# Order of weight loads and gate stores on the loading queue of an eight-expert feed-forward stage

## The reference

```python
xn = _layernorm(x, axis=-1)
s  = _L1_attn_ref(xn, wq, bq, wk, bk_, wv, bv, wo, bo)
gate = einsum('becd,edf->becf', xn, w1)      # 8 experts, d = 256, f = 704
up   = einsum('becd,edf->becf', xn, w3)
out  = einsum('becf,efd->becd', silu(gate) * up, w2)
x = x + s * silu(out)
```

## Time and profile before

| | us |
|---|---|
| median of 3 runs | 2246.42 |
| the 3 runs | 2246.42, 2250.37, 2243.02 |
| span of the profiled execution, first to last instruction | 2244.4 |
| TensorE matmul busy | 1996.7 (89%) |
| VectorE, ScalarE, GpSimd busy | 1538.4, 1396.0, 685.8 |

### The profile page before, as it was taken

How to read it: one execution, slowest core, us unless ns; L and a number is a source line. 1 busy time by engine, 2 the same in 40 slices (tenths; PEclk the granted TensorE clock), 3 DMA queues, 4 the chain that set the end, 5 groups by cost and what they waited for, 6 DMA issues and landing times. The chain is left out here.

```text
span 2244.4 us, 41413 instructions
## 1 busy us (share of the span) xinstructions
PE 1996.7 (89%) x12160; PEld 1485.8 (66%) x12160; DVE 1538.4 (69%) x3292; ACT 1396.0 (62%) x3261; POOL 685.8 (31%) x1032
## 2 busy tenths in 40 slices
PE   2999999999999999999999777787499999999997
PEld 1777768767777687687777566676355566656653
DVE  5886885877858858858778543232477777777773
ACT  3675675675756756757667544333267877777784
POOL 0343443433433434434434213233200210111012
PEclk9999999999999999999999888899699999999999
DMA  6000000000000000000000271211200110110001
GB/s 216 1 0 19 0 0 19 0 0 19 0 10 10 0 19 0 0 19 0 0 10 0 85 273 50 96 53 55 92 19 1 48 42 5 47 47 15 32 28 38
DMA packets 52360, 76.87 MB, mean 34 GB/s; under 512 B 1856, under 2 KB 42688, under 8 KB 51776
## 3 DMA queue, kind: packets, MB, share of 16 engines
q1 hardware_dynamic: 51744, 75.05, 9.7%
q10 hardware_dynamic: 544, 1.05, 0.2%
HBM read 55.12 MB, written 20.97 MB: 34 GB/s over the span
## 5 line engine op out<-in xcount | busy, mean ns | idle before, releaser
L1539 DVE TENSOR_REDUCE nm<-ps 128x1 f32<-128x512 f32 x512 | 336.9, 687 | 114.1 <-PE ps L1398 110.2
L826 POOL TENSOR_SCALAR pr<-pr,rinv 128x128 f32<-128x128 f32 (+3 forms) x512 | 262.8, 532 | 409.4 <-DVE rinv L700 409.4
L1650 ACT ACTIVATE pt<-pst 128x512 f32<-128x512 f32 x512 | 296.1, 602 | 142.0 <-PE pst L1406 140.9
L557 ACT ACTIVATE pr<-sc,nmax 128x128 f32<-128x128 f32 (+3 forms) x512 | 263.7, 530 | 88.0 <-DVE nmax L689 88.0
L832 POOL TENSOR_TENSOR qk<-ra,rb 128x256 f32<-128x256 f32 x256 | 195.3, 774 | 275.2 <-DVE rb L713 236.3
L1398 PE MATMUL ps<-kb,qb 96*128 96x512 f32 x512 | 238.0, 467 | 12.5 <-DVE nm L1539 10.0
L404 PE MATMUL w<-ident,pr 128*128 128x128 f32 x1280 | 194.3, 286 | 41.2 <-DVE qs L720 25.6
L689 DVE TENSOR_REDUCE nmax<-sc 128x1 f32<-128x128 f32 (+3 forms) x512 | 216.4, 482 | 19.9 <-PE sc L392 19.7
L390 PE MATMUL sc<-k,qs 128*128 128x256 f32 (+2 forms) x512 | 212.3, 416 | 12.4 <-DVE k L727 11.2
L1406 PE MATMUL pst<-qb,kb 128*128 128x512 f32 x512 | 208.0, 408 | 6.7 <-ACT pt L1650 3.6
L404 PEld LDWEIGHTS w<-ident,pr 128*128 128x128 f32 x1280 | 139.7, 144 | 81.7 <-DVE qs L720 43.4
(11 more groups left out here) (207 smaller groups left out, 5079.3 us busy)
## 6 DMA issues: line engine op xcount, KB each, us to landing
raw<-in_w SPq DMA_DIRECT2D x16, 704.0 KB, 8.0
raw<-in_w SPq DMA_DIRECT2D x8, 640.0 KB, 6.5
xa<-in_x SPq DMA_DIRECT2D x2, 2048.0 KB, 13.7
x<-in_x SPq DMA_DIRECT2D x8, 512.0 KB, 3.5
x_scratch<-x SPq DMA_DIRECT2D x8, 512.0 KB, 3.6
xt_hi_scratch<-xt_hi SPq DMA_DIRECT2D x1, 4096.0 KB, 14.7
xt_lo_scratch<-xt_lo SPq DMA_DIRECT2D x1, 4096.0 KB, 23.5
gate_scratch<-go SPq DMA_DIRECT2D x32, 128.0 KB
```

The lines of the kernel that those rows point to most:

```text
L557: act.activation(pr[:, h, SOFF[i]:SOFF[i] + (i + 1) * P], sc[:, bank, at:at + (i + 1) * P], ACT.Exp, bias=nmax[:, h, i:i + 1], accum_out=r ...
L826: pool.tensor_scalar(p, p, rinv[:, h, i:i + 1], 1.0, ALU.mult, ALU.mult).then_inc(scaled, 1)
L1539: dve.tensor_reduce(nm[:, g % 2, i, h:h + 1], ps[:, i % 2, :], AXX, ALU.max, negate=True).then_inc(max_done, 1)
L1650: act.activation(pt[:, g % 2, h, i, :], pst[:, i % 2, :], ACT.Exp).then_inc(exp_done, 1)
```

## The change

In the loop of the loading queue the two calls change places. For each e from 0 to 5 SyncE now issues the weights of expert e+2 first (with the four waits of `load13` and `load2` ahead of them) and the four stores of expert e second. The loads and stores, their waits, their sizes and all other engines' programs stay as they are.

```diff
                 sp.dma_start(io.xt1_lo, c.xt1_lo[:].bitcast(F32)).then_inc(xt_stored, 16)
                 with sp.Fori(0, E1 - 2) as e:
+                    load(e + 2)
                     store(e)
-                    load(e + 2)
                 store(E1 - 2)
                 store(E1 - 1)
                 sp.wait_ge(g_stored, 16 * NT * E1)
```

## The result

The changed kernel takes 2187.89 us (median of 4 runs, 2186.28 to 2188.42), the kernel before 2244.72 us beside it (2240.6 to 2250.37): a ratio of 0.974, with a 95% interval of 0.973 to 0.976. The forecast was 2185.4 us, with a range of 2180 to 2193.

The account below looks back on a forecast made before the run. The prediction took TensorE in experts 1 to 6 to be held by w1's load queued behind four stores; removing that gains 61.0 us, other terms cost 0: 2246.4 - 61.0 = 2185.4 us, range 2180 to 2193.

Parts of the forecast that it names:

- What bounds the kernel: Experts 1 to 6: ScalarE's first w1 cast (L1006) waits for a load behind four stores, stopping TensorE 47.6 us.
- When the load leaves: L944 of load(e+2) issues when w3 of expert e+1 is split, at 1322.8 instead of 1336.96.
- When it lands: Raw w1 tile for experts 1 to 6: between 3.9 and 11.31 us after issue, upper end taken, so 1334.1.
- e = 0, behind the stores of xt1: First load(e+2), while xt1 is still being stored: lands between 1333.0 and 1340.4; cost 0, at most about 0.2 us.
- The HBM figure of 358 GB/s: Objection for e = 0: 2.66 + 1.44 MB would take 11.5 us and land at 1334.2, the sum unchanged.
- The 3.64 us that TensorE bears: A cast starting by 1340.27, against ScalarE ready at 1336.63, does not stop TensorE in block 4.
- The stores behind the loads: The 24 loop stores (L965) finish by 1346, ScalarE needs them (L1026) at 1355.4: cover 9 us.
- slower rival: Stores behind 2.1 MB of loads hold ScalarE at L1026; one period late costs 94 us less 61: 2279; chance 0.02.
- The number of engines: Gate stores use 2 DMA engines, their slowest dimension, agreeing with DMA share 0.13, 2.1 of 16 engines.
- The sum: Expert 0's go to expert 6's go: 210.93 less six periods of 24.98 us gives 61.05 us gained.
- The second count: Cross-check over six experts: TensorE's idle 47.6 us plus 15 us of block 4 at lower clock makes 63.
- The median: Whole kernel: 2246.4 - 61.0 = 2185.4 us, the median lying 2.0 above the profiled span.

Follow-up runs that it names:

- experiment with wide stores: Kernel before the change, old order, each gate store cut into two DMAs with slowest dimension 64 instead of 2: 2207.08 us, ratio 0.983.
- second trace: The changed kernel with no edit, timed and traced again: 2180.41 us, ratio 0.971.

## Why the prediction was right

- *What bounds the kernel.* The wait of ScalarE for the raw tile behind the stores: shown, by the move of L944 and L945 alone giving the whole gain and the move of L953 and L954 alone nearly none.
- *When the load leaves.* 0.2 us after w3's split, as put down.
- *When it lands.* I took the upper bound of 11.3 us. Load(3) took 5.8 us from the issue of L944 to the landing of L945 (1350.43 + 5.3 - 1349.93), 11.4 in the kernel before. The old 11.3 us contained 4.9 us that came with the stores' slow transfer (experiment with wide stores). The sum did not depend on it.
- *e = 0, behind the stores of xt1.* Cost 0: no wait at the cast of 1338.46. But the load took 10.5 us from issue to landing here and 13.4 in the second trace, where it landed 0.1 us before the cast; behind that lay only the 3.6 us that TensorE bears. The HBM figure of 358 GB/s in the Trainium skill, DMA: Bandwidth & Descriptors (Specifications), did not bind here: 395 GB/s over the 7 us in which both moved.
- *The 3.64 us that TensorE bears.* Confirmed to 0.01 us by the load held until block 1.
- *The stores behind the loads.* Through at about 1371 in expert 1's case (from the window above), asked for at 1382.31: 11 us of cover; I had 9. Holding them for 10 us more cost nothing, for 16 us more 10 us in all. The slower rival's price was too high: I counted every us by which the stores hold ScalarE as paid, and of the 31 us that they held it there a third was paid.
- *The number of engines.* That a store with a slowest dimension of 2 runs on 2 engines (the same page of the Trainium skill, Why a DMA increments its semaphore by 16 and not by 1) fits the share of 0.13 in both kernels and the wide stores' earlier end. Their share of 0.34 is that of 5.4 of the 16 engines, so more than 2 carried them; the exact number of engines no run shows.
- *The sum.* 61.05 us forecast for the six periods, 61.13 in the trace. The clock came back in full, so what is left beside the 47.6 us of stops, 13.5, is its share. The second count had 15 for it, since it took expert 1's block for all six: from TensorE's restart to the clock's rise it was 5.3 us there and 3.1 to 6.1 in the six, 25.3 in all at a clock of 0.50, worth some 12.7.
- *The median.* 2185.4 forecast; 2187.89 and, again, 2180.41 measured. The first lies 2.5 us above, the second 5.0 below, 0.4 us inside the low end of the range: the range, drawn from three runs of one measurement, was narrow for two, and that both fell into it is in part luck. No term of the sum was mis-sized.

## What to carry to other kernels

Where a queue issues both loads for the future and stores of the present, look not only at when a load is issued but at what stands ahead of it in the transfer: a store that moves at 44 GB/s held a load of 1.44 MB up for 4.9 us after its issue. Put the transfer first whose waits are met first and whose reader is in the critical engine's chain; then ask for each wait how much of it the critical engine feels, since of ScalarE's waits at its first cast 3.6 us per expert were free and the rest was paid in full, at times with the clock on top, while of its waits before go a third was paid. And try stores whose slowest dimension is large, above all for the last one before a barrier: here that alone shortened the stage's end by 6.8 us.

## What the runs showed of the hardware that I had not expected

- How long TensorE stopped does not tell whether its clock falls. Behind stops of 2.00 and 3.56 us it stayed at 2.4 GHz; behind one of 2.96 us it fell to 1.2 GHz 1.3 us after TensorE had begun again; behind 2.04 and 3.37 us it began at 1.2 GHz. What decides between them no run separates.
- The same program began expert 0 at half clock in one trace and at full clock in another, worth 2.9 us.
- A DMA's issue is not of a fixed length on SyncE: L944 took 1.80 us behind four stores and 0.41 us without them; behind eight wide stores it took 0.78 us.
